# Eight instead of six weight tiles per accumulation group in the down projection of an attention and feed-forward kernel

## The chip, the cores and the metric

The kernel runs on the 8 cores of one Trainium2 chip. The cores share nothing but memory: each computes its own rows. The time is the device time of the slowest core, in microseconds (us). The engines of a core are PE (TensorE), DVE (VectorE), ACT (ScalarE), POOL (GpSimd) and SP (SyncE, which here only issues DMAs). A name with a q (SPq, POOLq) is the sequencer of that engine.

## The reference

x has shape (2, 8192, 1024). One layer is computed:

```python
xn = _layernorm(x, axis=-1)
# attention: 16 heads of 64, one shared k and v of 64 columns
latent = xn @ Wc_down                       # 1024 -> 512
q = (latent @ Wq_up).reshape(Bsz, Tlen, 16, 64)
kv = latent @ Wkv_up; k, v = kv[..., :64], kv[..., 64:]
att = softmax(where(causal, einsum('bthd,bsd->bhts', q, k) / 8, -inf))
s = einsum('bhts,bsd->bthd', att, v).reshape(Bsz, Tlen, 1024) @ Wc_proj
# feed-forward, weights are int32 times 1/127
gate = einsum('bsd,hd->bsh', xn, wg); up = einsum('bsd,hd->bsh', xn, wu)
ffn = einsum('bsh,dh->bsd', silu(gate) * up, wd)   # hidden 3072
x = x + s * silu(ffn)
```

## The kernel before

Each core takes one of the two sequences and every fourth chunk of 128 rows of it: 16 chunks of its own (e = 0 to 15), 2,048 rows. For each e it normalises four chunks of x, transposes them, computes k and v of them for itself, and runs causal attention of its own chunk e against 4(e + 1) tiles of 128 keys, in two groups of 8 heads (`emit_attn_hg`, L541). For one tile t the matmuls of the scores (L567) go to PSUM ps_sc, ACT takes the exponential (L578) into p_sb, POOL multiplies the last four tiles with a mask (L586), and the matmuls of tile t - 1 with v (L554) follow. ps_sc and p_sb have two buffers each. Over the kernel there are 1,088 such tiles.

All other work is put between these tiles. After each tile `pump` (L936) is called once and emits one piece: an obligatory one (transposes L373, k and v L424, q L468 and L483, the attention epilogue, the projection L644) or a lazy one. The only lazy work is the feed-forward part, a Python generator `gen_ffn_half` (L711) that emits its next piece when it is asked and then yields. If both kinds wait, lazy work gets every second call; if no work waits, the tile stands alone. Each engine executes its instructions in the order of emission. At the end of each attention group `flush_epi` (L989) emits all that is due at once.

A half block covers 256 own rows (two chunks). There are 8 of them, called half blocks 0 to 7 here (B = 0 to 3, `half` = 0 and 1), each entered in the lazy queue when attention of an odd e begins. It emits

- 24 pieces (FM = 3072 / 128 = 24), each with 8 matmuls for gate (L725) and 8 for up (L732), tanh on ACT (L736), and two products on DVE (L739, L743) into h_sb;
- then the "down" stage: for each half nh of the 1,024 output columns, groups of GM tiles of the hidden dimension, each tile with one matmul for each of the two chunks (L796: h_sb 128x128 as weights, wd_t 128x512 as moving operand), accumulated in ps_u, two banks of 512 columns. After a group DVE copies (L810, first group) or adds (L814) the two banks into o_sb in f32, and the generator yields;
- then, for each of the two chunks, the combination with attention and x (L830 to L844).

ps_u is a single buffer of two banks, shared by all but the attention tiles: its next user waits for the eviction of the last one by the token `st["util"]`. The first matmul of each group (mi == 0) waits for the evictions of the group before.

wd_t has 7 slots of 128x512 bf16. `wd_load` (L762) loads tile number seq (0 to 47 in a half block) into slot seq % 7; seven are issued before the first group, and the load of seq + 7 is emitted behind the matmuls of seq and waits for them (wd_war). In half blocks 0 and 1 (B = 0) the source is the int32 weight, converted by a DMA that POOL issues. In half block 0 each tile is also written back as bf16 to a buffer in DRAM by a DMA that SP issues (emit_wb), and the slot is reused only when that has landed. From half block 2 on the source is this bf16 copy, and SP issues the loads.

Of the kernel before, what the change touches and what calls it, by code (L numbers as in the profile page):

```python
# [115 lines left out]
def build_program(cfg: Cfg):  # L116
    nc = bass.Bass("TRN2", target_bir_lowering=False)
    T, D, NH, HD, LAT, FH = cfg.T, cfg.D, cfg.NH, cfg.HD, cfg.LAT, cfg.FH
    J, S, DK, LK, FM, QC = cfg.J, cfg.S, cfg.DK, cfg.LK, cfg.FM, cfg.QC
# [91 lines left out]
    with es:  # L211
# [499 lines left out]
        def gen_ffn_half(B, half):  # L711
# [8 lines left out]
            for m in range(FM):  # L720
# [31 lines left out]
                    pend[m + 3] = load_gu(m + 3, par, first_wb, from_bf)  # L752
                if YIELDS:
                    yield
            GM = 6
            accs = []
            for tc in range(2):
                eidx = 4 * B + 2 * half + tc
# [27 lines left out]
            for nh in range(2):  # L786
                for g4 in range(FM // GM):
                    gtoks = []
                    for mi in range(GM):
                        m = g4 * GM + mi  # L790
                        seq = nh * FM + m
                        sl_ = seq % 7
                        tdm = wd_toks.pop(seq)
                        for tc in range(2):
# [4 lines left out]
                                wd_t[:, sl_, :],  # L799
                                start=(mi == 0), stop=(mi == GM - 1)),  # L800
                                [tdm, h2_toks[m], st["util"] if mi == 0 else None],
# [180 lines left out]
        for e in range(S):  # L982
            if e + 1 < S:
                enqueue_group(e + 1)
            if e % 2 == 1:
                k = (e - 1) // 2
                tq_lazy.append(lambda B=k // 2, hf=k % 2: gen_ffn_half(B, hf))
# [128 lines left out]
```

How the kernel before makes its waits and increments, by code:

```python
            def body(eng):  # L71
                seen = {}
                for _, emit, waits, inc_sem, inc_by in ops:
                    per = {}
                    for t in waits:
                        k = id(t.sem)
                        if k not in per or per[k][1] < t.val:
                            per[k] = (t.sem, t.val)
                    for k, (sem, val) in per.items():
                        if seen.get(k, -1) >= val:
                            continue
                        if ename == "tensor" and self._producers.get(k) == {"tensor"}:
                            seen[k] = max(seen.get(k, -1), val)
                            continue
                        eng.wait_ge(sem, val)
                        seen[k] = val
                    ins = emit(eng)
                    if inc_sem is not None:
                        ins.then_inc(inc_sem, inc_by)
```

## Time and profile before

| | us |
|---|---|
| timed executions | 3169.03, 3204.01 |
| median of the two | 3186.52 |
| profiled execution | 3155.12 |
| its slowest core, first to last instruction | 3153.2 |
| its fastest core | 3120.5 |

The profile is of the slowest core (core 1). In its tables busy time is the sum over the instructions of an engine; the time for which an engine sat idle ahead of a group of instructions is put down to what released it last. "Issue" is time in which an engine waited for nothing that the profile shows. The granted clock is the share of TensorE's full clock (2.4 GHz): 1.00 or 0.50 at a given moment, between them as a mean over a stretch.

### The profile page before, as it was taken

Reading aid. Unit: us, or ns where it says so; the run is one execution under the profiler, and the core shown is the slowest. Engines: PE = TensorE matmul, PEld = TensorE weight load, DVE = VectorE, ACT = ScalarE, POOL = GpSimd, SP = SyncE. Lnnn points to the kernel's source line nnn. Section 1 sums busy time; section 2 is a strip of 40 time slices with the busy share of each in tenths; the row PEclk is TensorE's granted clock in tenths of the full one; section 3 lists DMA queues with packets and bytes.
Section 4 is the critical chain, followed back from the end, with each engine's and each line's share of the span. In section 5 each row is a group of like instructions: output and inputs, shape, how many; then the busy total and the mean of one; then the engine's idle time right before and its main releaser. Section 6 shows DMA issues by size and latency. Waiting matters only on the chain.

```text
span 3153.2 us, 32984 instructions; the slowest of 8 cores (3120.5 to 3153.2 us)
## 1 busy us (share of the span) xinstructions
PE 2056.7 (65%) x10464; PEld 988.6 (31%) x10464; DVE 1169.2 (37%) x1852; ACT 1308.5 (41%) x1457; POOL 416.6 (13%) x329
## 2 busy tenths in 40 slices
PE   1334546556575785875668667597585887688885
PEld 1112323222332342532235232252221542223521
DVE  4645444243434436335243341522512331511211
ACT  0111222222332433443634446346365437475465
POOL 0211122223243101110201101010011011011011
PEclk7556767688797896997879878799687998898988
DMA  5132274949586262450025300262011350012600
GB/s 97 30 49 50 43 108 51 152 95 152 66 88 130 57 150 84 109 143 23 21 63 137 85 30 15 55 148 82 15 29 34 82 149 21 23 28 60 150 26 14
DMA packets 547254, 232.12 MB, mean 74 GB/s; under 512 B 476432, under 2 KB 532752, under 8 KB 547088
## 3 DMA queue, kind: packets, MB, share of 16 engines
q1 hardware_dynamic: 429760, 186.88, 23.4%
q0 software_dynamic: 117328, 43.14, 12.7%
q8 instruction: 91, 1.49, 0.2%
q14 instruction: 75, 0.61, 0.1%
HBM read 241.62 MB, written 27.26 MB: 85 GB/s over the span
## 4 chain that ended last, share of the span: by engine, by line
PE 41%; DVE 20%; ACT 12%; DMA 11%; issue 10%; POOL 5%; DVEq 1%; ACTq 0%; SPq 0%; POOLq 0%
ACT p_sb L578 10%; PE ps_y L554 9%; PE ps_sc L567 9%; PE ps_u L725 5%; PE ps_u L732 5%; PE ps_u L796 5%; POOL p_sb L586 4%; DVE recbf L606 4%; DMA wu_t<-wu 3%; DMA xt<-xb 2%; PE ps_u L644 2%; DVE xnT L380 2%; DVE h_sb L743 2%; DMA wd_t<-wd 2%; DVE stat L306 2%
## 5 line engine op out<-in xcount | busy, mean ns | idle before, releaser
L578 ACT ACTIVATE p_sb<-ps_sc 128x1024 bf16<-128x1024 f32 x1088 | 1090.4, 1023 | 1282.2 <-PE ps_sc L567 1275.1
L554 PE MATMUL ps_y<-p_sb,vaug_sb 128*65 128x512 bf16 x2176 | 727.6, 419 | 256.9 <-POOL p_sb L586 152.9
L567 PE MATMUL ps_sc<-qs,kT_sb 65*128 65x512 bf16 x2176 | 729.1, 420 | 16.2 <-DVE qs L534 16.2
L586 POOL TENSOR_TENSOR p_sb<-p_sb,masks_sb 128x1024 bf16<-128x1024 bf16 x128 | 276.9, 2173 | 2228.2 <-ACT p_sb L578 2228.0
L554 PEld LDWEIGHTS ps_y<-p_sb,vaug_sb 128*65 128x65 bf16 x2176 | 208.7, 118 | 687.4 <-issue 607.4
L373 PE MATMUL ps_u<-ident_sb,xn_t 128*128 128x128 bf16 x512 | 65.8, 272 | 412.9 <-DVE xn_t L336 231.5
L567 PEld LDWEIGHTS ps_sc<-qs,kT_sb 65*128 65x128 bf16 x2176 | 220.2, 106 | 217.6 <-issue 71.1
L725 PE MATMUL ps_u<-xnT_own,wg_t 128*128 128x256 bf16 x1536 | 219.5, 290 | 81.8 <-DVE h_sb L743 57.9
L596 DVE CAST yf<-ps_y 64x1024 bf16<-64x1024 f32 x32 | 38.8, 1214 | 543.9 <-PE ps_y L554 543.8
L732 PE MATMUL ps_u<-xnT_own,wu_t 128*128 128x256 bf16 x1536 | 217.9, 289 | 24.4 <-DMA wu_t<-wu 24.3
L796 PE MATMUL ps_u<-wd_t,h_sb 128*128 128x512 bf16 x768 | 190.8, 393 | 60.2 <-DVE o_sb L814 28.6
L739 DVE SCALAR_TENSOR_TENSOR th<-t_sb,ps_u 128x256 bf16<-128x256 f32 x192 | 80.9, 421 | 395.0 <-ACT t_sb L736 394.5
L606 DVE RECIPROCAL recbf<-rec 1x1024 bf16<-1x1024 f32 x32 | 209.4, 6544 | 1.0
L725 PEld LDWEIGHTS ps_u<-xnT_own,wg_t 128*128 128x128 bf16 x1536 | 149.0, 103 | 183.5 <-issue 155.9
L373 PEld LDWEIGHTS ps_u<-ident_sb,xn_t 128*128 128x128 bf16 x512 | 47.6, 122 | 473.9 <-issue 466.6
L736 ACT ACTIVATE t_sb<-ps_u,cst 128x256 f32<-128x256 f32 x192 | 91.0, 474 | 225.0 <-PE ps_u L732 128.3
L732 PEld LDWEIGHTS ps_u<-xnT_own,wu_t 128*128 128x128 bf16 x1536 | 158.4, 104 | 54.8 <-issue 28.1
L315 ACT ACTIVATE xn_t<-xt,stat 128x1024 bf16<-128x1024 f32 x64 | 73.4, 1147 | 201.2 <-DVE stat L309 197.0
L796 PEld LDWEIGHTS ps_u<-wd_t,h_sb 128*128 128x128 bf16 x768 | 70.3, 100 | 178.9 <-issue 116.8
L814 DVE TENSOR_TENSOR o_sb<-o_sb,ps_u 128x512 f32<-128x512 f32 x96 | 61.7, 684 | 161.9 <-PE ps_u L796 158.5
L380 DVE CAST xnT<-ps_u 128x1024 bf16<-128x1024 f32 x64 | 78.3, 1223 | 88.8 <-PE ps_u L373 88.6
L644 PE MATMUL ps_u<-wproj_sb,yT 128*128 128x512 bf16 x256 | 75.6, 437 | 54.0 <-DMA yT<-ytmp 52.5
(86 smaller groups left out, 1229.8 us busy)
## 6 DMA issues: line engine op xcount, KB each, us to landing
wg_t<-wgbf SPq DMA_DIRECT2D x144, 256.0 KB, 3.7
wu_t<-wubf SPq DMA_DIRECT2D x144, 256.0 KB, 4.0
wd_t<-wdbf SPq DMA_DIRECT2D x288, 128.0 KB, 2.7
xt<-xb SPq DMA_DIRECT2D x64, 512.0 KB, 5.0
wg_t<-wg POOLq DMA_DIRECT2D x48, 256.0 KB, 7.8
wu_t<-wu POOLq DMA_DIRECT2D x48, 256.0 KB, 9.2
wd_t<-wd POOLq DMA_DIRECT2D x96, 128.0 KB, 5.0
xo_t<-xo SPq DMA_DIRECT2D x16, 512.0 KB, 4.6
```

The lines of the kernel that those rows point to most:

```text
L373: mts.append(O("tensor", lambda e, c=c: e.matmul(ps_u[:, c * 128:(c + 1) * 128], xn_ap[:, c * 128:(c + 1) * 128], ident_sb[:, :], start=Tr ...
L380: ev = O("vector", lambda e: e.tensor_copy(dst_ap, ps_u[:, :].rearrange("p (k n) -> p k n", k=DK)), [mts[-1]], out="v")
L554: last = O("tensor", lambda e_, t=t, nh=nh, par=par: e_.matmul(ps_y[0:65, nh * 512:(nh + 1) * 512], vaug_sb[:, t, :], p_sb[:, par, nh * 51 ...
L567: sct = O("tensor", lambda e_, t=t, nh=nh, sb2=sb2: e_.matmul(ps_sc[:, sb2 * 1024 + nh * 512:sb2 * 1024 + (nh + 1) * 512], kT_sb[0:65, t * ...
L578: ex = O("scalar", lambda e_, sb2=sb2: e_.activation(p_sb[:, sb2, :], ps_sc[:, sb2 * 1024:(sb2 + 1) * 1024], AF.Exp), [sct, st["p_war"][sb ...
L586: mtoks[t] = O("gpsimd", lambda e_, pview=pview, mj=mj: e_.tensor_tensor(pview, pview, masks_sb[:, mj, :].unsqueeze(1).broadcast_to([128, ...
L606: return e_.reciprocal(recbf[64:65, :], rec[64:65, :])
L644: pms.append(O("tensor", lambda e_, k=k, nh=nh, spar=spar: e_.matmul(ps_u[:, nh * 512:(nh + 1) * 512], yT[:, spar, k, :], wproj_sb[:, k, n ...
L725: gm = O("tensor", lambda e_, k=k, par=par, tok0=tok0: e_.matmul(ps_u[:, 0:256], wg_t[:, par, k, :], xnT_own[:, k, tok0:tok0 + 256], start ...
L732: um = O("tensor", lambda e_, k=k, par=par, tok0=tok0: e_.matmul(ps_u[:, 512:768], wu_t[:, par, k, :], xnT_own[:, k, tok0:tok0 + 256], sta ...
L736: tha = O("scalar", lambda e_: e_.activation(t_sb[:, :], ps_u[:, 0:256], AF.Tanh, scale=cst[:, 0:1]), [gm, t_consts, st["tsb_war"]], out="sc")
L796: mi=mi, g4=g4: e_.matmul(ps_u[:, tc * 512:(tc + 1) * 512], h_sb[:, m, tc * 128:(tc + 1) * 128], wd_t[:, sl_, :], start=(mi == 0), stop=(m ...
```

## The change

One line. GM, the number of hidden tiles in an accumulation group, is 8 where FM is divisible by 8, else 6. FM is 24 here. The loops over g4 and mi, the loads, and the ring of 7 slots stand as they were.

```diff
--- before.py
+++ after.py
@@ -752,7 +752,7 @@
                     pend[m + 3] = load_gu(m + 3, par, first_wb, from_bf)
                 if YIELDS:
                     yield
-            GM = 6
+            GM = 8 if FM % 8 == 0 else 6
             accs = []
             for tc in range(2):
                 eidx = 4 * B + 2 * half + tc
```

## Rows read from the trace of the kernel before

**Rows 1.** The page: busy time by engine (share), and the chain by engine.
```profile
PE 2056.7 (65%) x10464; PEld 988.6 (31%) x10464; DVE 1169.2 (37%) x1852; ACT 1308.5 (41%) x1457; POOL 416.6 (13%) x329
...
PE 41%; DVE 20%; ACT 12%; DMA 11%; issue 10%; POOL 5%; DVEq 1%; ACTq 0%; SPq 0%; POOLq 0%
```

**Rows 2.** The page's groups: operation, count | busy us, mean ns | idle before, releasers.
```profile
L796 PE MATMUL ps_u<-wd_t,h_sb 128*128 128x512 bf16 x768 | 190.8, 393 | 60.2 <-DVE o_sb L814 28.6 <-DVE o_sb L810 15.7 <-DMA wd_t<-wd 9.8
...
L814 DVE TENSOR_TENSOR o_sb<-o_sb,ps_u 128x512 f32<-128x512 f32 x96 | 61.7, 684 | 161.9 <-PE ps_u L796 158.5
```

**Rows 3.** Timeline, half block 2: start, us, operation, count [idle before it and releaser].
```profile
1160.82 2.75 PE L796 MATMUL ps_u<-wd_t,h_sb 128*128 128x512 bf16 x12 [1.09 <-DVE o_sb L810]
1161.49 6.97 SPq L768 DMA_DIRECT2D wd_t<-wdbf  x12
...
1163.41 0.60 PE L567 MATMUL ps_sc<-qs,kT_sb 65*128 65x512 bf16 x2
...
1163.68 1.28 DVE L814 TENSOR_TENSOR o_sb<-o_sb,ps_u 128x512 f32<-128x512 f32 x2 [3.00 <-PE ps_u L796]
...
1165.11 2.75 PE L796 MATMUL ps_u<-wd_t,h_sb 128*128 128x512 bf16 x12 [0.67 <-DVE o_sb L814]
```

**Rows 4.** Timeline, attention alone after half block 5.
```profile
2176.77 1.94 ACT L578 ACTIVATE p_sb<-ps_sc 128x1024 bf16<-128x1024 f32 x2 [0.35 <-PE ps_sc L567]
...
2179.06 1.94 ACT L578 ACTIVATE p_sb<-ps_sc 128x1024 bf16<-128x1024 f32 x2 [0.35 <-PE ps_sc L567]
```

**Rows 5.** L768, single first loads (27 read), then half block 2's 48: landing times.
```profile
L768 SPq DMA_DIRECT2D wd_t<-wdbf x1: 319/319/319, 1156.8 to 1156.8; - x1
...
DMA to landing us min/median/max: 2.0/2.0/2.0
...
L768 SPq DMA_DIRECT2D wd_t<-wdbf x1: 320/320/320, 2996.3 to 2996.3; - x1
...
L768 SPq DMA_DIRECT2D wd_t<-wdbf x1: 319/319/319, 1386.6 to 1386.6; - x1
...
DMA to landing us min/median/max: 1.8/1.8/1.8
...
L768 SPq DMA_DIRECT2D wd_t<-wdbf x1: 320/320/320, 2987.7 to 2987.7; - x1
...
DMA to landing us min/median/max: 3.2/3.2/3.2
...
L768 SPq DMA_DIRECT2D wd_t<-wdbf x48: 319/381/987, 1150.5 to 1185.7; - x48
...
DMA to landing us min/median/max: 2.0/2.7/4.3
```

**Rows 6.** Busy time by stretch (last three: clock, DMA share, GB/s); then chain pieces.
```profile
932.10:977.60 45.50, 34.60 (x131) 11.35 (x132) 10.49 (x16) 8.72 (x9) 21.72 (x41) 0.96 0.94 132
711.00:741.60 30.60, 18.59 (x61) 5.99 (x62) 11.38 (x8) 3.15 (x4) 14.26 (x23) 0.78 0.82 137
...
1156.10:1190.30 34.20, 28.35 (x126) 11.89 (x127) 9.01 (x15) 7.64 (x8) 0.00 (x0) 1.00 0.62 176
...
713.82 4.77 issue
...
933.82 5.29 DMA wd_t<-wd
939.10 0.14 issue
939.24 0.59 PE ps_u L796 x2
```

**Rows 7.** Timeline, half block 0, PE and POOL; then L768's landing there.
```profile
650.67 2.75 PE L796 MATMUL ps_u<-wd_t,h_sb 128*128 128x512 bf16 x12
...
651.87 3.29 POOL L768 DMA_DIRECT2D wd_t<-wd  x6 [39.17 <-PE ps_u L796]
...
680.18 2.12 POOL L586 TENSOR_TENSOR p_sb<-p_sb,masks_sb 128x1024 bf16<-128x1024 bf16 x1 [7.63 <-ACT p_sb L578]
682.25 3.24 POOL L768 DMA_DIRECT2D wd_t<-wd  x6
...
L768 POOL DMA_DIRECT2D wd_t<-wd x41: 528/528/599, 651.9 to 733.8; - x41
...
DMA to landing us min/median/max: 4.2/4.9/6.6
```

**Rows 8.** PE's busy time by stretch: us, busy, clock, DMA share, GB/s.
```profile
685.00:688.00 3.00, 0.21 (x1) 0.87 1.05 145
688.00:690.00 2.00, 2.00 (x6) 0.50 1.21 222
...
939.00:941.00 2.00, 1.65 (x6) 1.00 1.17 177
```

## The prediction

> **What bounds the kernel now.** I read the page's busy shares and the chain that ended last first, then the groups of instructions, then the timeline around the line that the change touches. No engine is full: PE is busy for 65% of the span and ACT for 41% [rows 1]. The chain is PE for 41%, and after it DVE, ACT, DMA and "issue" [rows 1]. So the time is a sum over stretches in which first one and then another engine waits, and the change must be priced in its own stretches. These are the second projection of the feed-forward part ("down" stage), L796: 768 matmuls, 190.8 us of modelled busy time, 60.2 us of idle PE ahead of them, of which 44.3 (28.6 + 15.7) were ended by an eviction of the group before (L814, L810), and 9.8 by a weight load [rows 2]. The 9.8 are loads of the int32 weights, which only the first two half blocks use. VectorE is busy for 61.7 us in the 96 adds of L814 [rows 2].
>
> In a half block of B > 0 the down stage is regular [rows 3]: 12 matmuls start at 1160.82, the attention matmuls of one tile follow at 1163.41 (so 12 matmuls hold PE for 2.59 us, 0.216 each), the two evictions run from 1163.68 for 1.28 us, and the next group starts at 1165.11. A group's period is 4.29 us, that is 2.59 for matmuls and 1.70 for the hand-over, of which attention's four matmuls fill 0.86 and PE is idle in 0.67. Eight periods make one half's stage.
>
> Where nothing is interleaved, attention alone takes two tiles per 2.29 us, 1.145 us a tile: the pairs of activations start at 2176.77 and at 2179.06 [rows 4]. ACT and the matmul-exp-matmul loop set that pace. So an attention tile that stands between two down groups costs less there than alone, since the evictions' time covers it.
>
> **The change part by part.** FM is 24, so GM becomes 8: a group is 16 matmuls, and there are 6 groups in a half instead of 8 (48 over the kernel instead of 64). The matmuls stay 768. The adds of L814 fall from 96 to 64; at 684 ns [rows 2] that is 21.9 us less on DVE, but none of it counts by itself, since only the wait after each group reaches PE. What is on the path is the hand-over.
>
> *Removed hand-overs, half blocks 2 to 7.* Two per half, so 12 x 1.70 = 20.4 us less [rows 3].
>
> *Moved attention tiles.* Each removed group also removes a yield, so an attention tile that was covered by a hand-over now runs elsewhere. The lazy queue runs empty after each of these stages (pure attention follows), so the tile is added there at 1.145 us [rows 4]: 12 x 1.145 = 13.7 us more. The real gain is 6.7 us, a third of what the hand-overs suggest. Bounds: nothing, if such tiles fall under other work, to 13.7.
>
> *The eighth tile.* The ring wd_t has 7 slots. A group of 6 found all its tiles loaded or under way when it began. A group of 8 cannot: the load of its eighth tile writes the slot of its first and is released by that tile's second matmul. The first load after a group's start is issued 0.67 us after it (1160.82 to 1161.49) [rows 3]. In 27 groups of halves 2, 3, 6 and 7 that I read singly, that first load landed 1.8 to 3.2 us after its issue, 2.0 in the first of them (1156.8) and 2.0 in the last (2996.3) [rows 5]; the mean is 2.29. PE takes 0.14 us to start after a landing [rows 6]. It wants the eighth tile 14 x 0.216 = 3.01 us after the group's start. It waits, then, for landing - 2.20 us: nothing in most groups, 1.0 us in the worst, and 0.19 us as the mean of the 27. 36 groups x 0.2 = 7 us more, with the ends 0 and 36 x 1.0 = 36. Behind the waiting load on SP's queue stand only the next tiles' loads; the following group wants its first tile 5 us later, so nothing else is late. The rate asked for rises from 6 tiles in 4.29 us to 8 in about 5.3, 8% more; the queues ran at 62% share in that stage [rows 6], so I take the landing times as they are.
>
> *Half block 1 (932 to 978).* Here the loads are int32 to bfloat16 from POOL's queue, and the stage is bound by supply: DMA share is 0.94, and the chain runs load after load (5.29 us, then 0.14, then two matmuls) [rows 6]. 41 loads in 45.5 us will take as long in any grouping. Only the two displaced attention tiles add 2.3 us. Ends: -1.1 (as the halves above) and +8, if the ring drains at each of 6 groups for more than a microsecond.
>
> *Half block 0 (650 to 742).* Its groups stand apart, since obligatory work lies between them, and each now starts on a full ring and runs 12 matmuls in 2.75 us [rows 7]. The first load leaves POOL 1.20 us after the group starts (650.67 to 651.87) and lands in 4.9 us (median of 41, 4.2 to 6.6) [rows 7]. So PE waits 1.20 + 4.9 + 0.14 - 3.01 = 3.2 us in each of the four groups before the flush at 692: +12.9. In the third and fourth, a mask multiplication stands ahead of the loads on POOL (680.18 for 2.12 us, loads from 682.25 instead of 681.2) [rows 7]: +1 to 2 us each, +3. After idle PE stretches of this length the granted clock was seen at 0.50, the 1.2 GHz level, for some 3 us (688 to 690, after 3 us nearly idle), and at 1.00 after a shorter wait (939 to 941) [rows 8]; half speed for 3 us loses 1.5 us. I take +1 for each of four groups, +4. Against that, 32 of the 48 tiles are then done before the flush instead of 24. The stretch 711.0 to 741.6 held the other 24, was near its supply limit (DMA share 0.82, clock 0.78) and cost 30.6 us, of which 4.8 is a piece of the chain put down to "issue" at 713.82 [rows 6]; the rest is 1.07 us a tile. Eight tiles fewer there: -8.6; the same eight as plain matmuls before it: 8 x 0.43 = +3.4. Two displaced tiles: +2.3. Together +17. Ends: -1 (every wait falls under obligatory work that PE would have waited for anyway) and +30.
>
> By the Trainium skill ("DMA: Bandwidth & Descriptors", Anatomy of one DMA — SWDGE (gpsimd) path) one DMA of this kind takes about 2.0 us plus its bytes over 436 GB/s; for the 256 KB of int32 read, my estimate from that page is 2.6 us, the wait in half 0 would be 0.9 instead of 3.2 us, and the whole sum would come out about 9 us lower. The rows say 4.9, with eight cores at work.
>
> **Sum.** -20.4 + 13.7 + 7 + 2.3 + 17 = +19.6, say +20 us, 0.6%. The profiled execution, whose times these are, took 3155.1 us (its slowest core's span 3153.2); the two timed ones took 3169.0 and 3204.0, with median 3186.5. The three spread by 49 us, more than the sum, so I add it to their mean, 3176.1: **3196 us**. On the profiled execution alone it would be 3175, on the median 3206.
>
> **Rivals.**
> *No stall at all.* The eighth tile lands in time in all 36 groups (most of the 27 read would) and half 0's waits hide under its obligatory work. Then -20.4 + 13.7 - 1 - 1 = -9, 3167 us. For it: the median landing is at the threshold. Against: int32 loads at 4.9 us leave 3 us open. Chance 0.22.
> *Full gain.* The displaced attention tiles also cost nothing and each of 16 hand-overs is saved: 16 x 1.70 = -27, 3149 us. Against it stands the attention-only pace, which these tiles would have to beat. Chance 0.08.
> *The ring becomes the bound.* The eighth load lands late in every group of B > 0, because bursts of eight load the queues more than bursts of six. At the longest landing of any load in such a stage, 4.3 us [rows 5], PE waits 2.1 us, and if the clock then falls each time it loses 1.5 more: 36 x 3.6 = +130, with the other terms (-6.7 + 2.3 + 17) 3319 us, slower by 4%. It decides for "slower" from about 1.4 us of wait per group, a landing of 3.6 us in the mean. The rows have 2.29. Chance 0.06.
> *The order shifts.* Fewer yields bring each later step of the feed-forward queue forward by two to four tiles; a projection or a load of x could meet a mask or an eviction that it missed before. There are gaps of about 5 us on PE that no engine explains (713.82 [rows 6]); four of them more or fewer is +-20 around the forecast: 3176 to 3216. Chance 0.09. That the edit does nothing is excluded, since 24 is divisible by 8.
> Forecast: 0.55.
>
> **Range and chances.** 2% is 64 us, about what a measurement of this kernel can tell from no change. Forecast, no stall, order shift and full gain all lie within it and hold 0.94; a slow outcome has 0.06, of which I leave 0.04 beyond 2%, and 0.02 goes to faster by 2%, for which no mechanism here has enough microseconds. The range takes in the no-stall case, the executions' own spread (3155 to 3204) and the upper ends of terms 3 and 5 in part: 3150 to 3245.
>
> **What would show it.** L796 still 768 matmuls, but runs of 16, period about 5.2 us in 1156 to 1190; L814 x64; PE's waits for L814 and L810 down from 44 to about 33 us; PE's waits on wd_t from wdbf up from about 1 to some 7 us, from wd from 10 to 25 or more; the first half's groups at 6 us each instead of 2.75. I am wrong if the waits on wdbf come to more than 1 us a group, or if there are none in half 0, or if the attention tiles freed from the groups run in less than 1.1 us.

## The result, and the profile after

The changed kernel took 3175.1 us (median of 32 executions) against 3161.5 us (median of 31) for the kernel before on the same chips: ratio 1.0043, 95% interval 1.0027 to 1.0059. It is slower by 13.6 us. That is small against 2%, but well outside zero. Some executions run in a slower state, in which the cores of one die show a lower clock; the two medians above are of all executions, while this ratio, and every ratio and median of the experiments, is of executions outside that state.

The profiled executions differ by more, 3189.5 to 3153.2 us on their slowest cores. The first four cores ran at a granted clock of 0.804 here and 0.818 before (medians), so part of that difference is not the change's. On the other four the clock was the same (0.822), and their medians, 3156.6 and 3134.8 us, still lie 21.8 us apart: one pair of executions scatters by several microseconds. To see where the time goes I compare the same instruction in both traces: attention tile n (the n-th execution of L578, there are 1,088) does the same work in both. The table gives its start after minus its start before, as the median over the eight cores.

| tile | start before (core 1) | what lies around it | after - before, us |
|---|---|---|---|
| 80 | 611 | ahead of half block 0's down stage | +3.3 |
| 98 | 683 | its third group | +13.8 |
| 100 | 710 | end of the attention group, flush | +21.6 |
| 107 | 748 | behind half block 0 | +16.6 |
| 224 | 1208 | behind half blocks 1 and 2 | +20.0 |
| 324 | 1518 | behind half block 3 | +23.9 |
| 728 | 2410 | behind half blocks 4 and 5 | +19.1 |
| 1087 | 3121 | last tile | +25.2 |

13.3 us arise between tiles 80 and 107, in half block 0. (Fewer yields bring work forward: at tiles 98 and 100 the changed kernel has emitted 12 and 16 more matmuls of the down stage, 2.6 and 3.5 us, and at 107 16 gate and up matmuls more, some 1.7 us. At 80, 224 and after, both have emitted the same work.) The rest is spread out; how far a single profile can be trusted for it is said below.

These are the page's and the grouped rows of the changed kernel (core 0), which answer to [rows 1, 2]:

```profile
PE 2102.3 (66%) x10424; PEld 1008.1 (32%) x10464; DVE 1136.6 (36%) x1820; ACT 1311.7 (41%) x1457; POOL 414.1 (13%) x329
...
L796 PE MATMUL ps_u<-wd_t,h_sb 128*128 128x512 bf16 x744 | 193.5, 408 | 60.7 <-DMA wd_t<-wd 22.5 <-DVE o_sb L814 20.0 <-DVE o_sb L810 9.4
...
L814 DVE TENSOR_TENSOR o_sb<-o_sb,ps_u 128x512 f32<-128x512 f32 x64 | 41.1, 684 | 147.6 <-PE ps_u L796 147.5
```

(24 matmul records are missing from this core's trace; the weight loads are all there, x768.) The adds are 64 instead of 96, and DVE is busy for 20.6 us less in them. The idle time ahead of L796 is what it was, 60.7 against 60.2 us, but its releasers have changed places: evictions 44.3 to 29.4, the int32 weight loads 9.8 to 22.5. The change has traded one wait for another.

The regular stage of half block 2, which answers to [rows 3]:

```profile
1181.58 3.64 PE L796 MATMUL ps_u<-wd_t,h_sb 128*128 128x512 bf16 x16 [0.67 <-DVE o_sb L814]
1186.77 3.61 PE L796 MATMUL ps_u<-wd_t,h_sb 128*128 128x512 bf16 x15 [0.67 <-DVE o_sb L810]
1191.92 3.67 PE L796 MATMUL ps_u<-wd_t,h_sb 128*128 128x512 bf16 x16 [0.67 <-DVE o_sb L814]
```

A period is 5.15 to 5.19 us for 16 matmuls, where 4.29 stood for 12: the hand-over is still 1.70.

Half block 0, PE and then POOL, which answers to [rows 7]:

```profile
646.09 2.97 PE L796 MATMUL ps_u<-wd_t,h_sb 128*128 128x512 bf16 x13
652.66 1.01 PE L796 MATMUL ps_u<-wd_t,h_sb 128*128 128x512 bf16 x2 [3.61 <-DMA wd_t<-wd]
...
692.68 0.59 PE L796 MATMUL ps_u<-wd_t,h_sb 128*128 128x512 bf16 x2 [2.02 <-DMA wd_t<-wd]
...
701.70 1.03 PE L554 MATMUL ps_y<-p_sb,vaug_sb 128*65 128x512 bf16 x2 [7.13 <-POOL p_sb L586]
```

```profile
688.62 3.77 POOL L768 DMA_DIRECT2D wd_t<-wd  x7
698.88 0.53 POOL L768 DMA_DIRECT2D wd_t<-wd  x1 [6.49 <-DMA wdbf<-wd_t]
699.43 4.20 POOL L586 TENSOR_TENSOR p_sb<-p_sb,masks_sb 128x1024 bf16<-128x1024 bf16 x2
```

On this core each of the four groups ahead of the flush stops before its last two matmuls, those of the eighth tile, for 3.6 us in the first; that one is the longest, the other seven cores waited 1.3 to 2.2 us there. The second fence shows what I had not seen coming: the last of the eight loads behind the third group wants the slot of the eighth tile, which itself came late and is still being written back to DRAM. POOL waits 6.5 us for that, with two attention masks behind the load in its queue, and PE waits 7.1 us for the masks. Before, the same wait was 3.8 us on cores 0 and 1 (here core 1) and 2.7 on the other six:

```profile
687.78 0.61 PE L554 MATMUL ps_y<-p_sb,vaug_sb 128*65 128x512 bf16 x1 [3.77 <-POOL p_sb L586]
```

Over the eight cores its median went from 2.7 to 7.2 us. The edit touches only the grouping of PE's matmuls and DVE's adds; the wait travels over SP's write-back, POOL's load and POOL's mask.

### The profile page after: what moved, and what is told of

It reads as the page before. It is cut to its first block, busy times and chain, and to the rows that moved or that the text cites. A ratio compares the mean times of both kernels' runs of the same rounds, so it can differ in the third digit from the quotient of the medians.

```text
span 3189.5 us, 32881 instructions; the slowest of 8 cores (3139.9 to 3189.5 us)
## 1 busy us (share of the span) xinstructions
PE 2102.3 (66%) x10424; PEld 1008.1 (32%) x10464; DVE 1136.6 (36%) x1820; ACT 1311.7 (41%) x1457; POOL 414.1 (13%) x329
## 4 chain that ended last, share of the span: by engine, by line
PE 43%; DVE 18%; DMA 12%; ACT 11%; issue 10%; POOL 5%; DVEq 1%; ACTq 0%; SPq 0%; POOLq 0%
PE ps_y L554 11%; PE ps_sc L567 10%; ACT p_sb L578 10%; PE ps_u L725 5%; PE ps_u L732 5%; POOL p_sb L586 5%; PE ps_u L796 4%; DVE recbf L606 4%; DMA wu_t<-wu 3%; DMA xt<-xb 2%; PE ps_u L644 2%; DVE xnT L380 2%; DVE stat L306 2%; DMA wd_t<-wd 2%; ACT xn_t L315 1%
## 5 line engine op out<-in xcount | busy, mean ns | idle before, releaser
L578 ACT ACTIVATE p_sb<-ps_sc 128x1024 bf16<-128x1024 f32 x1088 | 1094.0, 1022 | 1311.8 <-PE ps_sc L567 1298.1
L554 PE MATMUL ps_y<-p_sb,vaug_sb 128*65 128x512 bf16 x2176 | 748.3, 429 | 255.5 <-POOL p_sb L586 155.0
L567 PE MATMUL ps_sc<-qs,kT_sb 65*128 65x512 bf16 x2176 | 745.5, 428 | 16.2 <-DVE qs L534 16.2
L725 PE MATMUL ps_u<-xnT_own,wg_t 128*128 128x256 bf16 x1536 | 228.8, 299 | 74.4 <-DVE h_sb L743 45.3
L732 PE MATMUL ps_u<-xnT_own,wu_t 128*128 128x256 bf16 x1536 | 228.8, 299 | 24.0 <-DMA wu_t<-wu 24.0
L796 PE MATMUL ps_u<-wd_t,h_sb 128*128 128x512 bf16 x744 | 193.5, 408 | 60.7 <-DMA wd_t<-wd 22.5
L796 PEld LDWEIGHTS ps_u<-wd_t,h_sb 128*128 128x128 bf16 x768 | 73.4, 103 | 180.2 <-issue 130.4
L743 DVE TENSOR_TENSOR h_sb<-th,ps_u 128x256 bf16<-128x256 bf16 x192 | 80.9, 422 | 66.2 <-PE ps_u L732 36.7
```

What stands on the lines that cost most here:

```text
L554: last = O("tensor", lambda e_, t=t, nh=nh, par=par: e_.matmul(ps_y[0:65, nh * 512:(nh + 1) * 512], vaug_sb[:, t, :], p_sb[:, par, nh * 51 ...
L567: sct = O("tensor", lambda e_, t=t, nh=nh, sb2=sb2: e_.matmul(ps_sc[:, sb2 * 1024 + nh * 512:sb2 * 1024 + (nh + 1) * 512], kT_sb[0:65, t * ...
L578: ex = O("scalar", lambda e_, sb2=sb2: e_.activation(p_sb[:, sb2, :], ps_sc[:, sb2 * 1024:(sb2 + 1) * 1024], AF.Exp), [sct, st["p_war"][sb ...
L725: gm = O("tensor", lambda e_, k=k, par=par, tok0=tok0: e_.matmul(ps_u[:, 0:256], wg_t[:, par, k, :], xnT_own[:, k, tok0:tok0 + 256], start ...
L732: um = O("tensor", lambda e_, k=k, par=par, tok0=tok0: e_.matmul(ps_u[:, 512:768], wu_t[:, par, k, :], xnT_own[:, k, tok0:tok0 + 256], sta ...
L796: mi=mi, g4=g4: e_.matmul(ps_u[:, tc * 512:(tc + 1) * 512], h_sb[:, m, tc * 128:(tc + 1) * 128], wd_t[:, sl_, :], start=(mi == 0), stop=(m ...
```

## The experiments

Each was timed beside the kernel before, with 12 executions (8 of g8_ring11, 6 of g12_ring11). The theories: **A**, the eighth tile finds no slot in a ring of 7, and since an int32 load and its write-back are slow this costs in half blocks 0 and 1; **B**, the yields that fall away cost, because attention tiles lose their cover or the order shifts; **C**, the eighth tile is late in half blocks 2 to 7 too.

**Where.** Three kernels apply the groups of 8 to some half blocks only.

```diff
-            GM = 6
+            GM = 8 if B == 0 else 6                 # g8_early
+            GM = 8 if B > 0 else 6                  # g8_late
+            GM = 8 if B == 0 and half == 0 else 6   # g8_half0
```

> Groups of 8 in half blocks 0 and 1 only (int32 loads), 6 elsewhere. Theory A (the eighth tile's load, 4.9 us from issue to landing, comes late in these two half blocks, and masks queue behind it on POOL): nearly all of the loss is here, +10 to +16 us against the kernel before, ratio 1.003 to 1.005. Theory B (what costs is the removed yields: attention tiles that no longer stand beside a hand-over): only 4 of 16 yields are removed here, so +3 us. Theory C (the eighth tile's late load in half blocks 2 to 7): 0.

> Groups of 8 in half blocks 2 to 7 only, 6 in 0 and 1. Theory A: near zero, since the two removed hand-overs per half (-20.4 us in all), the displaced tiles (+13.7) and 36 short waits (+7) cancel: -3 to +3 us, ratio 0.999 to 1.001. Theory B: 12 of the 16 yields, +10 us, ratio 1.003. Theory C: +13 us, 1.004.

> Groups of 8 in half block 0 alone. Theory A: half block 0 carries the loss, +12 us, ratio 1.004, since half block 1 (long stretches bound by supply) gives a little back: with groups of 8 in both it was 1.0035. If half block 1 had its part, +5 us.

Measured: g8_early 1.0035 (1.0003 to 1.0068), g8_late 1.0008 (0.9976 to 1.0039), g8_half0 1.0054 (1.0034 to 1.0074). The loss lies where A puts it: g8_half0 has all of it and removes only 2 of the 16 yields, for which B would have a microsecond or two. The other two alone would not decide: g8_late removes 12 yields and costs nothing that can be seen, but B's 1.003 is still inside its interval and C's 1.004 just outside. In the traces tile 80 to tile 107 gives +12.3 us in g8_early, +13.6 in g8_half0 and -0.6 in g8_late. Half block 1 cannot be told from zero.

**The ring.** The room for more slots comes from tensors that live on different partitions: recbf (row 64) into ytmp (rows 0 to 63), and for 11 slots yf and ytmp into rec.

```diff
-    wd_t = sbuf("wd_t", [128, 7, 512], BF16)
+    wd_t = sbuf("wd_t", [128, 9, 512], BF16)    # and each 7 of the ring's bookkeeping
-    recbf = sbuf("recbf", [128, HGW], BF16)
+    recbf = ytmp
```

> Groups of 8 everywhere, with a ring of 9 slots instead of 7 (recbf shares the memory of ytmp, other partitions, to make room). The eighth tile is then under way when its group starts. Theory A: the waits on wd_t and their clock losses go in the first two half blocks, and what is left is the gain: -5 to -9 us against the kernel before, ratio 0.997 to 0.998. Theory B: the ring changes nothing, +10 to +14 us as in the changed kernel. Theory C: as A.

> The control of the last one: groups of 6 as before, ring of 9 slots. All theories: 0 to -3 us (the two slots let the first half block's stage prefetch 2 tiles more, its PE waits on wd_t of about 10 us shrink a little), ratio 0.999 to 1.000.

> Groups of 8 with a ring of 8 slots (recbf in ytmp's memory). Theory A: it is the step from 7 to 8 that counts, since with 8 slots a whole group is loaded or under way at its start: -10 to -18 us against the kernel before, most of the way from 1.0043 to the 0.9935 of nine slots. Rival D (more loads in flight help by themselves, each slot about the same): halfway, about -3 us, ratio 0.999.

> Groups of 8, ring of 11 slots: one size changed against the kernel with 9. Theory A (a whole group has to fit, and half block 1 is held by how many loads are in flight): a little faster than with 9, by 0 to 4 us, in half block 1 alone; ratio 0.992 to 0.995. Rival (bytes per us are the limit there): same as with 9.

| | groups of 6 | groups of 8 |
|---|---|---|
| 7 slots | 1 | 1.0043 (1.0027 to 1.0059) |
| 8 slots | | 0.9988 (0.9961 to 1.0015) |
| 9 slots | 0.9971 (0.9943 to 1.0000) | 0.9935 (0.9904 to 0.9966) |
| 11 slots | | 0.9948 (0.9922 to 0.9974) |

This is the main result. Groups of 8 lose with 7 slots and win with 9: two slots turn +13.6 us into about -20. B wanted no effect of the ring. The same two slots give groups of 6 about 9 us, more than the 0 to 3 that I expected. With 8 slots the kernel took 3153.1 us, with 9 3143.4, with 11 3139.7 (medians). In the times it is D (each slot about the same) that foretold the 8 slots: 0.999, measured 0.9988. A's -10 to -18 us (0.9968 to 0.9943) reaches only the edge of the interval, and the ninth slot seems to add as much again as the eighth. The traces show both a step and a slope. The table has the time from the first to the last weight load of L796 and PE's waits for wd_t, as medians over the eight cores of one execution each:

| | before | changed | g6, 9 slots | g8, 8 slots | g8, 9 slots | g8, 11 slots |
|---|---|---|---|---|---|---|
| half block 0, us (of it waits) | 90.1 (5.5) | 96.7 (11.2) | 85.4 (2.3) | 81.6 (0) | 81.6 (0) | 81.5 (0) |
| half block 1, us (of it waits) | 47.2 (6.4) | 45.5 (8.4) | 41.2 (3.2) | 40.3 (5.1) | 38.2 (3.8) | 35.6 (3.2) |
| half blocks 2 to 7 together, us (of it waits) | 206.3 (0.8) | 194.2 (4.8) | 204.5 (0) | 183.4 (0.6) | 182.2 (0) | 181.8 (0) |

In half block 0 the eighth slot does everything, as A says: the waits are gone on all eight cores. In half block 1 each slot more helps, as D says. In half blocks 2 to 7 the eighth slot takes off 11 us more (6 to 8 if g8_late and g8_pad are taken for the 7 slots, with 191.1 and 189.2), so a part of what 7 slots cost lay there too, as C had it. For the ninth slot the stages give 3 us and the two ratios some 17, with an uncertainty of 13; that stays open. PE on core 5 with 9 slots runs the third and fourth group of half block 0 without a stop, and the wait for the masks is that of the kernel before again (2.67 us here, 2.66 on the same core there; 7.70 with groups of 8 and 7 slots):

```profile
662.98 4.92 PE L796 MATMUL ps_u<-wd_t,h_sb 128*128 128x512 bf16 x16 [0.61 <-DVE q2m L506]
...
671.87 0.59 PE L554 MATMUL ps_y<-p_sb,vaug_sb 128*65 128x512 bf16 x2 [2.67 <-POOL p_sb L586]
672.30 5.30 PE L796 MATMUL ps_u<-wd_t,h_sb 128*128 128x512 bf16 x16
```

With 8 slots the groups are whole as well:

```profile
660.12 4.63 PE L796 MATMUL ps_u<-wd_t,h_sb 128*128 128x512 bf16 x16
...
669.97 4.85 PE L796 MATMUL ps_u<-wd_t,h_sb 128*128 128x512 bf16 x16
```

Sixteen matmuls in 4.6 and 4.9 us instead of 3.6 are the clock and not a wait: in these two stretches PE is busy throughout and the granted clock is 0.76 and 0.73 (columns as in [rows 6]):

```profile
660.00:664.60 4.60, 4.57 (x18) 1.82 (x18) 0.42 (x1) 0.35 (x1) 4.11 (x5) 0.76 0.24 46
670.00:674.60 4.60, 4.60 (x17) 1.84 (x16) 2.96 (x6) 0.00 (x0) 2.29 (x3) 0.73 0.92 210
```

**The masks behind the load.** For chunk 4, first 8 heads, the masks go to DVE.

```diff
-                    mtoks[t] = O("gpsimd", lambda e_, ...: e_.tensor_tensor(
+                    on_dve = (e == 4 and hg == 0)
+                    mtoks[t] = O("vector" if on_dve else "gpsimd", lambda e_, ...: e_.tensor_tensor(
```

> The changed kernel (groups of 8, ring of 7) with the four mask multiplications of one attention group (chunk 4, first 8 heads) on DVE instead of POOL. They stand behind the weight loads of half block 0 on POOL's queue, one of which waits 6.6 us for the write-back of the eighth tile's slot. Theory A1 (POOL's queue, blocked by that wait, delays the masks and so PE by some 7 us): 4 to 7 us faster than the changed kernel, ratio to the kernel before 1.002 to 1.003, and the delay of attention tile 100 against tile 98 goes from 8 us to 2 to 4. Theory A2 (only PE's own waits for the eighth tile cost): no change, 1.0043.

> The control: the kernel before (groups of 6) with the same four masks on DVE. There the masks wait little on POOL's queue: A1 expects 0 to -3 us (PE's 3.8 us wait for a mask at 684 shrinks), A2 expects 0.

Measured: 1.0040 (1.0018 to 1.0063) with groups of 8, 0.9988 (0.9965 to 1.0010) with groups of 6. The time does not confirm A1, whose 1.002 to 1.003 is still inside the interval. The trace (core 5; with the added line, L796 is L797 here) shows what happens:

```profile
679.63 0.59 PE L554 MATMUL ps_y<-p_sb,vaug_sb 128*65 128x512 bf16 x2 [1.19 <-DVE p_sb L587]
680.06 2.45 PE L797 MATMUL ps_u<-wd_t,h_sb 128*128 128x512 bf16 x10
682.70 0.59 PE L797 MATMUL ps_u<-wd_t,h_sb 128*128 128x512 bf16 x2 [0.18 <-DMA wd_t<-wd]
686.05 0.59 PE L797 MATMUL ps_u<-wd_t,h_sb 128*128 128x512 bf16 x2 [2.77 <-DMA wd_t<-wd]
687.94 1.01 PE L797 MATMUL ps_u<-wd_t,h_sb 128*128 128x512 bf16 x2 [1.29 <-DMA wd_t<-wd]
```

The wait for the masks is gone (7.70 us to 1.19), but PE, arriving 6.5 us earlier at the fourth group, now waits 4.2 us for the same slots' loads; tile 98 to tile 100 still loses 5.9 us against 7.8. Over the whole stage the picture is better for A1. On the eight cores (medians) the wait for the masks falls by 6.1 us and the waits for the loads of half block 0 rise by 3.0, from 11.2 to 14.2; the stage lasts 91.3 us against 96.7 in the changed kernel, and tile 80 to tile 107 loses 3.8 us where it lost 13.3 (-0.4 with groups of 6 and the same edit). So about half of the masks' wait comes back as waits for late slots, and the rest was a cost of its own: in the trace the edit saves at least the 4 to 7 us that A1 named. The two times, 1.0040 and 1.0043, differ by 1 us with an uncertainty of 9 and can neither show nor exclude it.

**The hand-over's price.** Groups of 4 and of 12.

```diff
-            GM = 6
+            GM = 4     # g4, ring of 7
+            GM = 12    # g12_ring11, ring of 11
```

> Groups of 4, ring of 7: twelve groups a half, so 32 hand-overs and 32 yields more than before. If a hand-over costs 1.70 us and covers one attention tile worth 1.145, it adds 0.55 x 32 = +18 us, ratio 1.0055, and a stage of half blocks 2 to 7 takes 12 x (1.72 + 1.70) = 41 us instead of 33.5. If the tiles covered are worth the whole hand-over: 0 us.

> Groups of 12, ring of 11 slots (yf, ytmp in the memory of rec, other partitions). Four groups a half instead of eight. Theory A: in half blocks 2 to 7 the twelfth tile is wanted 22 x 0.216 = 4.75 us after the group's start and lands after about 3.1, so no wait; four hand-overs less per half against groups of 6 at 1.70 - 1.145 = 0.55 us net each, -13 us over six halves, and as much in the first two as with the ring of 9 (-9 us): -20 to -26 us against the kernel before, ratio 0.992 to 0.994. Rival: 12 loads in about 6.9 us (229 GB/s against 183 before) are more than the queues give, waits on wd_t from wdbf appear, ratio 0.996 to 1.000.

g4: 1.0007 (0.9984 to 1.0031), where I expected 1.0055. Stage by stage it is otherwise. The regular period is what the sum says, 1.72 + 1.70 (core 5):

```profile
1709.54 1.89 PE L796 MATMUL ps_u<-wd_t,h_sb 128*128 128x512 bf16 x8 [0.67 <-DVE o_sb L814]
...
1712.97 1.89 PE L796 MATMUL ps_u<-wd_t,h_sb 128*128 128x512 bf16 x8 [0.67 <-DVE o_sb L814]
```

and from tile 324 to the end, over half blocks 4 to 7, g4 loses 7.6 us, 1.9 per half against the 2.2 that 4 x 0.55 gives. But up to tile 324, over half blocks 0 to 3, it is 7.7 us ahead of the kernel before, where the sum had 4 x 2.2 us of loss. Why is not shown. That small groups spread the demand on the ring is not it: PE waited longer for the int32 loads, 16.2 us against 11.8 (medians of the eight cores). The price fits where it could be read, and the assumption that it holds in all eight halves was wrong or is hidden by the scatter of single profiles; the 18 us that I expected are excluded by the time.

g12_ring11: 0.9886 (0.9856 to 0.9916), 3121.0 us, the fastest of all, and more than the 0.992 to 0.994 expected. The rival (the queues can't give it) fell (core 5; L797 is L796, one line down):

```profile
1111.51 5.34 PE L797 MATMUL ps_u<-wd_t,h_sb 128*128 128x512 bf16 x24 [0.74 <-DVE o_sb L811]
1118.39 5.34 PE L797 MATMUL ps_u<-wd_t,h_sb 128*128 128x512 bf16 x24 [0.67 <-DVE o_sb L815]
...
1110.00:1130.00 20.00, 17.92 (x82) 7.74 (x81) 3.86 (x6) 3.07 (x3) 0.00 (x0) 1.00 0.84 230
```

24 matmuls without a stop, a period of 6.88 us (24 x 0.216 + 1.70), at 230 GB/s and a DMA share of 0.84. From tile 224 to the end it gains 9.6 us. The other 25.3 lie before tile 224; with groups of 8 and the same 11 slots only 15.3 do. Why 12 is better than 8 by ten microseconds there I have not separated. A group of 12 on 11 slots has one slot too few as well, like 8 on 7, and still PE's waits for wd_t are small: 4.9 us in half blocks 0 and 1 together (19.6 in the changed kernel, 11.8 before) and at most 0.8 in the others. A likely reason, by the sum in the expectation: the twelfth tile is wanted 4.75 us after the group's start and not 3.01, so its load has more time.

**The order of what follows.** Two empty yields after each half's groups put every later piece beside the tile at which it stood before.

```diff
+            yield
+            yield
             for tc in range(2):
                 eidx, par = accs[tc]
```

> The changed kernel (groups of 8, ring of 7) with two empty yields after each half's groups, so that from there on every piece stands beside the same attention tile as in the kernel before. Theory A: the order of what follows plays no part, and the time is that of the changed kernel, ratio 1.003 to 1.005. Rival (the shift by two to four tiles costs by itself, as masks, projections and transposes meet otherwise): back to 1.000 to 1.002.

Measured 1.0023 (1.0006 to 1.0040), between the two expectations; its interval overlaps that of the changed kernel. By the two ratios the order plays a part of 6 us, and by their intervals anything from none to 14. This stays open. A single profile doesn't settle it: g8_early and the changed kernel have the same instructions up to tile 200 (half block 2 comes behind it), and their traces stand at +16.1 and +25.3 there. Between tiles 80 and 107 they agree within 1.0 us. So the profile carries the reading of half block 0 and not of offsets of a few microseconds over longer stretches.

## Why the prediction was wrong, point by point

Two steps failed. The first is the last one, from the sum to the forecast. The sum was +20 us and the measured difference is +13.6, but I called 0.6% "no change" because I took the spread of the few executions (2% for a verdict) as the resolution. With some thirty executions on each side it is 0.16%, and a loss is what came. The sum pointed at slower, and the forecast should have said so. The second is the largest term of the sum, half block 0: the mechanism was right, the landing of the eighth tile was taken as 4.9 us where 3.3 was measured, and a wait on POOL's queue was not named at all (below).

The time, 3175.1 us, lies in the range, 21 us below my 3196. Of these, 14.6 come from the base (I took 3176.1, the mean of three executions with one of 3204; the kernel before is at 3161.5) and 6.4 from the sum. That the sum on the profiled execution alone gives 3175 is luck: that execution was 6.4 us faster than the median, and the sum 6.4 us too high.

- *Hand-overs, 12 x 1.70 = -20.4:* right. The period is 5.15 to 5.19 us, 3.45 + 1.70, and g4 and g12_ring11 give the same 1.70 at 8 and at 24 matmuls.
- *Displaced attention tiles, +13.7, and 36 short waits, +7:* right as far as can be measured. PE's waits for loads from wdbf are 4.7 us on core 5, 3.9 on core 0. What they cost is more: without them, with 9 slots, the six stages are 12.0 us shorter (194.2 to 182.2, table above), though in the traces of g8_late and g8_pad, also with 7 slots, they are longer by only 9 and 7 us. The three terms together were +0.3 us; g8_late gives 1.0008 +- 0.003, and its trace loses 1.6 us from tile 224 to the end. So the full gain and the ring as the bound in half blocks 2 to 7 are both out. Most of the 27 landings had said this.
- *Half block 1, +2.3:* not resolved, but its reason was wrong. I took a DMA share of 0.94 [rows 6] for a limit in bytes. With 9 slots the stage of core 5 lasted 37.4 us instead of 46.4:

```profile
921.00:967.40 46.40, 35.27 (x132) 10.86 (x132) 10.50 (x16) 9.02 (x9) 21.71 (x41) 0.96 0.94 138
```

```profile
896.40:933.80 37.40, 28.98 (x117) 9.84 (x118) 6.43 (x10) 5.63 (x6) 20.68 (x39) 1.00 1.06 148
```

The first is the kernel before, the second g8_ring9 (columns as in [rows 6]). With 39 loads instead of 41 and two attention tiles fewer in the window, the rate still rose from 138 to 148 GB/s. Core 5 is not typical for groups of 6 with 9 slots (45.1 us there, 40.2 to 41.9 on the other seven). By the medians of the eight cores, 47.2 us before, groups of 8 alone take off 1.7, 9 slots alone 6.0, and both together 9.0 (table above): most of it is the ring.
- *Half block 0, +17:* the term that was mis-sized. Measured 12 to 14 us between tiles 80 and 107 in four traces (changed, g8_early, g8_half0, g8_pad). I took the median of all 41 loads, 4.9 us, as the landing of the eighth tile. But its load is the first that POOL issues after the group's start, and those first loads landed in 3.3 us in the first two groups, in the kernel before and after alike (medians of the eight cores; the core that I had read, core 1, had 4.5 and 4.2). With 3.3 my own line gives 1.20 + 3.3 + 0.14 - 3.01 = 1.6 us, and 1.4 and 1.5 were measured. The four waits ahead of the flush add up to 6.2 us in the median (3.6 + 1.5 + 2.0 + 0.15 = 7.3 on core 0) against my 12.9. In its place came the wait that I had not named: the write-back of the late tile holds its slot, the load behind it holds POOL, and PE waits 7.1 us for the masks where core 0 had waited 3.8 (+3.4; 2.7 to 7.2 in the median). I had asked what queues behind the waiting load on SP but on POOL only counted a mask ahead of it. Behind the flush, tiles 100 to 107 gave back 5.0 us, less than my 8.6. The fall of the clock was right in kind: the stop of 3.6 us that ends at 652.66 is followed by a granted clock of 0.50 from 652.6 to 658, the 1.2 GHz level.
- *No stall at all* (0.22) and *the order shifts* (0.09): the first is excluded, since PE stopped for the eighth tile in half block 0 and the time rose; the second is open, 6 us by the ratios and none to 14 by their intervals.

## What to carry to other kernels

An accumulation group and the ring that feeds it are one decision: with fewer slots than a group has tiles, the last tiles' loads wait for the group itself. That need not cost: 12 tiles on 11 slots did well, probably because a long group leaves its last load more time. What it costs depends on the slowest way in which a slot is filled and freed, here an int32 load with a write-back, and not on the regular stage; price the slowest stage and follow the queue of the engine that issues the load, since everything behind it there waits too. With two slots more the same edit changed sign (groups of 6 and 8 with 9 slots: 0.9971 and 0.9935), and with groups of 12 and 11 slots the kernel became 1.1% faster than before.

## What the runs showed of the hardware

- The loads that SP issues gave 230 GB/s (core 5) without PE once waiting for one in a stretch of 20 us (DMA share 0.84), with all eight cores at work, against 176 GB/s in the same stage before [rows 6].
- A DMA share of 0.94 was not a full pipe: with more slots and groups of 8 the same stage on the same core reached 1.06 and 148 GB/s. The share can pass 1, so it does not say how full the pipe is.
- How long an int32 load takes depends on its place and on the core more than on the grouping. The first load after a group's start landed in 3.3 us (median of eight cores, first two groups of half block 0), while the median of all 41 loads of a core is 4.8 to 5.6. On core 0 with groups of 8 these are

```profile
L768 POOL DMA_DIRECT2D wd_t<-wd x41: 528/528/592, 647.1 to 739.7; - x41
...
DMA to landing us min/median/max: 3.2/5.5/7.8
```

  and on the same core before 2.9/4.9/6.3; on core 5 they are 3.1/5.5/7.2 with groups of 8 and 3.2/5.5/7.4 before. The 4.2/4.9/6.6 of [rows 7] is core 1.
